# Value rows of the last attention visited two at a time

## What is computed

```python
def _L1_attn_ref(x, w_qkv):
    qkv = x @ w_qkv
    q, k, v = jnp.split(qkv, 3, axis=2)      # each reshaped to (B, H, T, D)
    att = jnp.einsum('bhqd,bhkd->bhqk', q, k) * scale
    att = jnp.where(causal, att, -jnp.inf)
    att = jax.nn.softmax(att, axis=-1)
    out = jnp.einsum('bhqk,bhkd->bhqd', att, v)
    return out.transpose(0, 2, 1, 3).reshape(B, T, C)
```

## Time and profile before

| | us |
|---|---|
| runs before: median of 3 | 1924.44 |
| lowest, highest | 1921.16, 1942.72 |
| span of the profiled execution | 1941.8 |
| PE busy, whole span | 1696.7 (87%) |
| DVE busy | 1296.8 (67%) |
| ACT busy | 1143.6 (59%) |
| POOL busy | 661.8 (34%) |
| mean granted clock of TensorE | 0.939 |

### The profile page before, as it was taken

The page is one execution under the profiler, slowest core; times in us unless marked ns, Lnnn a source line. Parts: engine busy times, 40 slices in busy tenths (PEclk is TensorE's granted clock), DMA queues, the critical chain, the costliest instruction groups (busy, mean ns, idle before and its releaser), DMA issues. The chain is left out here.

```text
span 1941.8 us, 38672 instructions
## 1 busy us (share of the span) xinstructions
PE 1696.7 (87%) x13334; PEld 704.4 (36%) x13334; DVE 1296.8 (67%) x2458; ACT 1143.6 (59%) x1788; POOL 661.8 (34%) x1227
## 2 busy tenths in 40 slices
PE   6878878597899999999999888886699999999886
PEld 4311212243343433434333555454333333333232
DVE  6677778574766666666662346665478888888254
ACT  6789999442055555555556433334327777777746
POOL 6465565575232222312222001104312222222464
PEclk9799999798899999999999998998659999999998
DMA  8533335168212312313210410001502222222201
GB/s 241 126 66 60 54 68 142 32 153 175 40 40 40 67 51 51 67 41 67 50 41 23 142 43 1 0 1 49 171 21 49 48 49 48 46 47 68 45 28 44
DMA packets 91800, 125.99 MB, mean 65 GB/s; under 512 B 24501, under 2 KB 63797, under 8 KB 91398
## 3 DMA queue, kind: packets, MB, share of 16 engines
q1 hardware_dynamic: 89526, 121.17, 27.2%
q10 hardware_dynamic: 2096, 2.47, 0.4%
HBM read 75.90 MB, written 47.58 MB: 64 GB/s over the span
## 5 line engine op out<-in xcount | busy, mean ns | idle before, releaser
L1059 ACT ACTIVATE q_buf<-ps 128x1024 f32<-128x1024 f32 (+1 forms) x1152 | 864.1, 822 | 453.3 <-PE ps L935 450.4
L1171 DVE TENSOR_REDUCE o_sb<-ps 128x1 f32<-128x512 f32 (+3 forms) x864 | 712.5, 865 | 248.1 <-PE ps L970 163.1
L1124 POOL TENSOR_SCALAR_AFFINE_SELECT q_buf<-q_buf 128x256 f32<-128x256 f32 x768 | 364.5, 499 | 768.6 <-ACT q_buf L1059 637.4
L992 PE MATMUL ps<-q_buf,v_buf 128*9 128x512 f32 (+7 forms) x4608 | 462.7, 497 | 59.8 <-POOL q_buf L1124 55.2
L935 PE MATMUL ps<-q_buf,k_buf 49*128 49x512 f32 (+3 forms) x1536 | 320.3, 518 | 0.0
L935 PE MATMUL ps<-q_buf 48*128 48x512 bf16 (+7 forms) x1536 | 261.8, 334 | 33.6 <-ACT q_buf L1059 26.7
L1231 DVE TENSOR_SCALAR q_buf<-q_buf 128x1024 f32<-128x1024 f32 x288 | 218.0, 765 | 57.1 <-ACT q_buf L1059 53.3
L992 PEld LDWEIGHTS ps<-q_buf,v_buf 128*9 128x9 f32 (+1 forms) x4608 | 95.1, 96 | 237.6 <-issue 118.2
L935 PEld LDWEIGHTS ps<-q_buf 48*128 48x128 bf16 (+1 forms) x1536 | 75.4, 94 | 283.7 <-ACT q_buf L1059 225.8
L935 PEld LDWEIGHTS ps<-q_buf,k_buf 49*128 49x128 f32 x1536 | 131.5, 188 | 125.8 <-ACT q_buf L1059 53.7
L456 PE MATMUL ps<-w_wg,identity 128*128 128x512 f32 (+1 forms) x214 | 108.6, 633 | 31.0 <-PEq L113 31.0
(11 more groups left out here) (183 smaller groups left out, 1565.8 us busy)
## 6 DMA issues: line engine op xcount, KB each, us to landing
q_buf<-qm_d SPq DMA_DIRECT2D x32, 384.0 KB, 6.5
qm_d<-pr_buf SPq DMA_DIRECT2D x80, 128.0 KB, 2.4
o_d<-pr_buf SPq DMA_DIRECT2D x16, 512.0 KB, 2.7
q_buf<-o_d SPq DMA_DIRECT2D x8, 1024.0 KB, 5.1
q_d<-q_buf SPq DMA_DIRECT2D x48, 128.0 KB, 2.1
k_d<-q_buf SPq DMA_DIRECT2D x48, 128.0 KB, 1.9
k_buf<-km_d SPq DMA_DIRECT2D x32, 192.0 KB, 6.6
q_buf<-q_d SPq DMA_DIRECT2D x60, 96.0 KB
```

Source lines behind the costliest of these rows:

```text
L992: mm = nc.tensor.matmul(ps[VW * j:VW * j + V_ROWS_OUT, o_bank + half % O_BUFS, lo * P:(lo + nq) * P], v, units(i, r, j)[:, 0, off * P:(off ...
L1059: nc.scalar.activation(units(i, g, WIDE * e, WIDE), ps[:, bank:bank + WIDE, :], ACT.Exp, scale=scale).then_inc(s_e, 1)
L1124: nc.gpsimd.affine_select(out=blk, in_=blk, compare_op=ALU.is_ge, fill=0.0, base=0, pattern=[[0, 2], [1, P]], channel_multiplier=-1)\
L1171: nc.vector.tensor_reduce(to, sc, AX_X, ALU.max).then_inc(s_mr, 1)
```

## The change

In a1 alone, PE no longer visits one value row behind each row of scores. `VALUES_BY_TWO` gives the value rows to visit behind row g, counted from -2 and -1 for rows 7 and 8 of the item before: two behind row 0 (7 and 8), two behind row 2 (0 and 1), one behind row 3 (2), two behind row 5 (3 and 4), two behind row 7 (5 and 6). Nothing is visited behind rows 1, 4, 6 and 8. The copies of finished halves move to `COPY_AT`: after the last exponential of row 1 (second half of the item before) and of row 4 (first half). The other two attentions keep their order (`VALUES_BY_ROW`). No product, exponential or copy is added or removed.

```diff
--- before.py
+++ after.py
@@ -63,6 +63,10 @@
     ((7, 4, 4, 4, 0),), ((8, 5, 5, 3, 0), (8, 7, 7, 1, 3)),
 )
 A_ROWS = 3
+
+
+VALUES_BY_ROW = {g: (g - 2,) for g in range(ROWS_P)}
+VALUES_BY_TWO = {0: (-2, -1), 2: (0, 1), 3: (2,), 5: (3, 4), 7: (5, 6)}
 
 
 MAX_ROWS = (
@@ -697,6 +701,9 @@
             V_ROWS_OUT = VW if latent else VS
             STORES = 1 if latent else QUAD + 1
             PLAG, PRING = 2, 4
+            by_two = has_max and not latent
+            VALUES_AT = VALUES_BY_TWO if by_two else VALUES_BY_ROW
+            COPY_AT = ((4, EXPS_R - 1), (1, EXPS_R - 1)) if by_two else ((A_ROWS + PLAG, 0), (PLAG, 0))
             M_WIDE, M_BUFS = (1, 3) if latent else (2, 2)
             M_PAIRS = 2 * ROWS_P
             REDUCES = UNITS // M_WIDE
@@ -1026,10 +1033,11 @@
                                 done = WIDE * (e + 1)
                                 if ahead is not None and done % 2 == 0:
                                     max_pair(n, b, i, *ahead, done // 2 - 1)
-                            if g >= PLAG:
-                                value_row(n, i, g - PLAG)
-                            elif last != 0:
-                                value_row(n - 1, i - 1, g - PLAG + ROWS_P)
+                            for v in VALUES_AT.get(g, ()):
+                                if v >= 0:
+                                    value_row(n, i, v)
+                                elif last != 0:
+                                    value_row(n - 1, i - 1, v + ROWS_P)
 
                     def rest():
                         for g in range(ROWS_P - PLAG, ROWS_P):
@@ -1058,10 +1066,10 @@
                                     act.wait_ge(s_pv, ROWS_P * n + g + 1 + (g - PRING == A_ROWS - 1) + BASE)
                                 nc.scalar.activation(units(i, g, WIDE * e, WIDE), ps[:, bank:bank + WIDE, :],
                                                      ACT.Exp, scale=scale).then_inc(s_e, 1)
-                                if has_max and e == 0:
-                                    if g == PLAG and last != 0:
+                                if has_max:
+                                    if (g, e) == COPY_AT[1] and last != 0:
                                         copy_output(b, i - 1, 1)
-                                    if g == A_ROWS + PLAG:
+                                    if (g, e) == COPY_AT[0]:
                                         copy_output(b, i, 0)
 
                     def first():
```

## The result

The changed kernel takes 1996.67 us (median of 4, 1989.25 to 2008.61); the kernel before 1922.8 (median of 4). The ratio is 1.0347, 95% interval 1.029 to 1.0405. That is 74 us where 23 were forecast, above the range of 1918 to 1973. The profiled execution spans 1995.0 us.

The account below looks back on a forecast made before the run. Bound: each row's fixed chain, PE's score unit 3 waiting for ACT's exponential 0. Items +1.36 us; 0.4 + 13 x 1.36 + 2 + 3 = 23 us on 1924.4 gives 1947.4 us, range 1918 to 1973.

Parts of the forecast that it names:

- The sign: Whole kernel: slower by more than about 1% had chance 0.54, within 1% 0.40, faster by over 1% 0.06.
- The chain: Last attention: row order of PE waiting for ACT lengthens each item from 25.08 us by 1.36; likeliest case, chance 0.45.
- the clock: Rival, rows 1, 2 or 4, 5: one visit per item at the lower clock, 20 us more, 1967 us; chance 0.22.
- Merged visits: Value visits on PE: 0.12 us saved four times an item, 0.48 us an item, 7.7 us in all.
- Rows without a visit: Rows 1, 4, 6, 8: ACT's slack is spent, so the following row's score unit 3 begins 3.13 us after their start.
- the copies in front of exponential 0: ACT, after rows 1 and 4: each moved copy adds 0.48 us to the chain, 0.96 us an item.
- DVE's 0.2 in row 7: Row 7: the second maximum pair waits for DVE's reduction and goes 0.2 us later than ACT would allow.
- Selects and other queues: POOL's selects, ring slots, SP's stores: covered or not waited for, priced 0; one pair of selects, 0.76, as upper bound.
- Ends: First and last items: item 0 +0.4 us, item 14 +2, item 15 +3.
- The chain's own range: Likeliest case: 1938 to 1957 us, from the merge's 7.7 us and DVE's 3 us off or on.
- The copies are hidden: Rival, rows 2 and 5: something later than ACT holds them, so 15 us less, 1932 us; chance 0.18.
- The gain case: Rival, score unit 3's wait for exponential 0: ACT's lag costs nothing, merge alone gains 7.7 us, 1916.7 us; chance 0.15.

Follow-up runs that it names:

- Filling all four stretches: Score products repeated in PE's idle time in all four stretches without values: changed kernel 1951.26 us (ratio 1.0137); changed kernel with copies put back 1939.39 us (1.0104).
- ACT held up: Kernel before, values behind every row, with further unused ACT copies ahead of exponential 0, two in row 2 and one in row 5: 1966.89 us, ratio 1.0214.

## Why the prediction was wrong

*The sign* was right, and the time lay above the range. The chain, which was worked out, held; the clock, which was a rival, decided.

*Merged visits.* Right. A visit of 1024 columns takes 1.84 us at a full clock (1658.39 to 1660.23). The 0.12 per visit was real, and too small to matter.

*Rows without a visit, and the copies in front of exponential 0.* Right in mechanism and size: 26.35 us an item measured, 26.44 forecast. The copies measured 0.81 instead of 0.96: with them back, the values of row 5 start late (3.81 instead of 3.65), since the second pair waits for DVE's last reduction of row 4, so some 0.15 of their time was covered. DVE's 0.2 in row 7 was about 0.1 (5.76 us for rows 6 and 7, 1648.74 to 1654.50, against 5.66 without the term).

*Selects and other queues*, priced 0. Right: an item's DVE and POOL times are as before (21.9 and 7.1 us), ACT's is 19.15 against 19.57, and no value row is seen to wait for POOL in the steady items.

*The clock.* This is the step that failed. The likeliest case took the granted clock of the steady items, 1.00, as given, and the rival "the clock falls" had a chance of 0.22 and a price of one fall an item at 1.24 us. Measured: 21 visits hit in 13 items, 1.6 an item, at 1.7 us each, since a fall costs more at a longer visit (3.41 instead of 1.84 us for 1024 columns) than at value row 3, from which I took the price: 36.3 us in these items. The prediction had seen both stretches: 4.4 us without values in rows 1 and 2 with about 1 us of idle PE (0.77 in the item shown), and the visit of value row 3 near the end, at 0.50. It weighed against them that other rows of the last item kept their level. That was a weak reason: the change made such a stretch at four places of each item, and visits behind three of them were hit.

*Ends.* 5 us were forecast; the last two periods grew from 24.83 and 20.22 us (copies at 1798.19, 1823.02 and 1843.24 before) to 31.00 and 28.38 (1837.89, 1868.89, 1897.27), 14 us. The granted clock in these two fell from 0.93 and 0.92 to 0.78 and 0.64, so most of it is the clock too. The beginning, up to the first copy behind row 1, grew by 3.4 us where 0.4 was forecast.

*The chain's own range*, 1938 to 1957, does not follow from the two terms named for it: 1947.4 - 3.2 is 1944, 1947.4 + 7.7 is 1955. The whole range does not hang on it.

*The rivals.* "The clock falls" was the true one, under-priced. "The copies are hidden" fell: they cost 13 us directly and, with the clock, 43. The gain case fell: unit 3 waits for exponential 0 in rows 2 and 5, which the gain case had denied. The Trainium skill ("TensorE: Matmul & The Clock Gate", section "A second HAM failure mode: psum-queue depth-cycling") says that frequent micro-idling between groups of matmuls makes the clock swing. The trace agrees in part: the swings between 1.00 and 0.50 went when the waits, recorded as 0.3 to 0.6 us of idle time each in the changed kernel, were filled; but the kernel before has waits of 0.34 us in its steady items and no swing.

What stays open is what exactly lets the clock fall. Neither the idle time of an item nor the length of a stretch without values nor missing values alone does it, by the table. Filling all four stretches removed the falls from the steady items of both kernels; but the repeated products add both time at work and matmuls, and no run parts the two. Nor is it known why 45 us of uninterrupted work ahead of the stage, in the profile before, ran at 0.50 throughout.

## What to carry to other kernels

When PE is nearly saturated, work moved away from a stretch can cost more than its own time: if what is left there lets the granted clock fall, the next block can run at half speed. Look first for rows of the same kernel in which PE has slightly less to do and the clock already falls, and count them as the likely case, not as an oddity. Read the clock and the length item by item: the shortest item gives the chain, the rest is the clock. Find the unit of a row that waits for the other engine (here score unit 3 for exponential 0), keep everything that need not come first (copies too) behind what it waits for, and use the wait for work that is ready. That was worth 15 us where each row had its visit. With merged visits it was no remedy: the work put ahead was itself waiting for DVE, and both kernels stayed 50 us above the one before.

## What was not expected of the hardware

- Repeating score products in idle time made the changed kernel faster: by 32 us with 7 extra products an item, by 45 us with twelve. Its steady items took 26.35 to 31.25 us, and 26.46 with all the repetitions (one took 26.68).
- In the items of the changed kernel shown, a fall cost 1.6 to 1.7 us each (26.35, 27.95, 29.66, 31.20). With single visits and ACT held up it cost 1.2 us, or 2.3 where two visits were hit.
- PE can be busy without a break and still stay at the lower level: 45 us at 0.50 ahead of the last attention in the profile before, where the profile after had 1.00.
- Two edits that cost 27 us (merge alone) and 3 us (copies alone) cost 74 together.
